# Attention of a decoder layer on one core: value products in pairs of groups, and an x load three groups later

## What is computed

```
x = layernorm(x + attention(x))          # 16 heads of 16, causal, w_qkv, w_proj
x = layernorm(x + slots(x, ctx_1024))    # 3 iterations of slot attention with a GRU cell
x = layernorm(x + experts(x))            # 16 experts of 64, the best 4 of them
```

```
qkv = x @ w_qkv + b_qkv                  # 16 heads, head dimension 16
att = einsum('bhqd,bhkd->bhqk', q, k) / 4, causal, softmax
y   = einsum('bhqk,bhkd->bhqd', att, v)
return y @ w_proj + b_proj
```

## Time and profile before

| | before |
|---|---|
| median of three runs | 658.3 us (658.2 to 659.8) |
| the profiled execution's own time | 656.96 us |
| its span (first to last instruction) | 655.2 us |
| TensorE busy | 616.9 us, 94% of the span |
| VectorE, ScalarE, GpSimd busy | 493.4, 327.1, 227.3 us |
| mean granted clock of TensorE | 0.993 of full speed |

### The profile page before, as it was taken

How to read it: one execution, slowest core, us unless ns; L and a number is a source line. 1 busy time by engine, 2 the same in 40 slices (tenths; PEclk the granted TensorE clock), 3 DMA queues, 4 the chain that set the end, 5 groups by cost and what they waited for, 6 DMA issues and landing times.

```text
span 655.2 us, 13948 instructions
## 1 busy us (share of the span) xinstructions
PE 616.9 (94%) x5048; PEld 561.9 (86%) x5064; DVE 493.4 (75%) x1039; ACT 327.1 (50%) x734; POOL 227.3 (35%) x274
## 2 busy tenths in 40 slices
PE   5889999999989899999999999999999997999996
PEld 5766787778768899999999999999988986999995
DVE  4755676666745888979888798897998988667663
ACT  5444645555664455664556645566466635131220
POOL 9502435233454431322323222232323114252542
PEclk9899999999999999999999999999999999899999
DMA  8645656457200400000000000000000000142250
GB/s 284 184 130 144 181 154 195 123 171 221 79 18 1 141 22 2 17 18 2 0 0 16 16 0 0 0 0 0 0 2 1 2 1 1 26 140 84 81 162 32
DMA packets 31374, 43.34 MB, mean 66 GB/s; under 512 B 3072, under 2 KB 18912, under 8 KB 31328
## 3 DMA queue, kind: packets, MB, share of 16 engines
q1 hardware_dynamic: 31328, 42.73, 21.5%
HBM read 29.39 MB, written 13.21 MB: 65 GB/s over the span
## 4 chain that ended last, share of the span: by engine, by line
PE 57%; DVE 15%; issue 13%; POOL 5%; DMA 4%; ACT 3%; SPq 2%; another core or an unknown queue 1%; DVEq 0%; POOLq 0%; ACTq 0%
PE bank L448 26%; PE bank L2163 11%; PE bank L1983 4%; POOL hid_hl L793 3%; PE bank L1883 2%; DMA k_rows<-k_hl 2%; PE bank L1841 2%; PE bank L1969 2%; PE bank L2000 1%; PE bank L456 1%; PE bank L1848 1%; PE bank L1864 1%; DMA k_op<-k_rows 1%; PE bank L1992 1%; DVE attn L1375 1%
## 5 line engine op out<-in xcount | busy, mean ns | idle before, releaser
L448 PE MATMUL bank<-slots_hl,whhT_hl 128*128 128x256 f32 x864 | 113.3, 284 | 0.0
L448 PEld LDWEIGHTS bank<-slots_hl,whhT_hl 128*128 128x128 f32 x864 | 105.7, 188 | 2.5 <-ACT gate_z L1096 1.0
L2163 PE MATMUL bank<-attn_hl,vg_hl 128*128 128x256 f32 x864 | 106.1, 281 | 0.2
L2163 PEld LDWEIGHTS bank<-attn_hl,vg_hl 128*128 128x128 f32 x864 | 101.2, 188 | 4.3 <-ACT attn_hl L807 3.9
L1285 DVE TENSOR_REDUCE neg_max<-bank 128x2 f32<-128x512 f32 (+1 forms) x96 | 65.5, 690 | 44.5 <-PE bank L1850 28.4
L862 ACT ACTIVATE pT<-bank 128x512 f32<-128x512 f32 x96 | 56.9, 598 | 47.2 <-PE bank L1864 31.6
L674 POOL TENSOR_SCALAR_AFFINE_SELECT pT<-pT 128x512 f32<-128x512 f32 x64 | 40.6, 638 | 107.3 <-ACT pT L862 107.2
L688 POOL TENSOR_TENSOR sq<-sq 128x256 f32<-128x256 f32 x24 | 18.1, 754 | 170.9 <-ACT sq L1081 130.4
L793 POOL TENSOR_TENSOR hid_hl<-hid,hid_hl 128x512 fp32r<-128x512 f32 x32 | 41.0, 1309 | 25.3 <-ACT hid_hl L807 25.2
L448 PE MATMUL bank<-values_hl,hid_hl 128*128 128x256 f32 x384 | 49.2, 286 | 0.3 <-DVE x L1559 0.3
L448 PE MATMUL bank<-x2T_hl,keys_hl 128*128 128x256 f32 x384 | 48.6, 284 | 0.0
(11 more groups left out here) (212 smaller groups left out, 1281.3 us busy)
## 6 DMA issues: line engine op xcount, KB each, us to landing
gate_rows<-gate_mem SPq DMA_DIRECT2D x48, 128.0 KB, 3.1
q_rows<-q_hl SPq DMA_DIRECT2D x21, 256.0 KB
k_rows<-k_hl SPq DMA_DIRECT2D x21, 256.0 KB
q_op<-q_rows SPq DMA_DIRECT2D x28, 192.0 KB, 3.2
k_op<-k_rows SPq DMA_DIRECT2D x14, 384.0 KB, 4.3
x_in<-in_x_dram SPq DMA_DIRECT2D x8, 256.0 KB, 6.6
c_in<-in_ctx_dram SPq DMA_DIRECT2D x8, 256.0 KB, 4.8
out_dram<-y_out SPq DMA_DIRECT2D x8, 256.0 KB, 2.8
```

The lines of the kernel that those rows point to most:

```text
L448: mm = pe.matmul(dst, left(a), right(b), start=first and n == 0, stop=last and n == 2, skip_group_check=True)
L2163: mm = pe.matmul(halves(b)[:, m, :], vg_hl[:, j, v_part, 3 * t + r, q:q + P], attn_hl[:, j, at_part, t, :], start=n == 2 and a + m + t == ...
```

## The change

On TensorE the value products of quads q and q + 1 (q even) are now both issued in third 1 of pass q + 2. Before, those of q came in third 2 of pass q + 1, and those of q + 1 in third 2 of pass q + 2. On SyncE the load of an even batch of x stands at place 3 of the period instead of place 0. On GpSimd the residual of an even batch stands at place 4 instead of place 3. Nothing else is changed, and the code's waits are the same.

```diff
@@ -559,7 +559,7 @@
                     write_q(period + 1, place // 2)
                 elif place in (1, 4) and 1 <= period + 1 < PAIRS:
                     write_k(period + 1, place // 4)
-                if place == 0 and 2 <= 2 * period < B:
+                if place == 3 and 2 <= 2 * period < B:
                     load_x(2 * period)
                 elif place == 5 and 2 <= 2 * period + 1 < B:
                     load_x(2 * period + 1)
@@ -737,7 +737,7 @@
                     text_lo(2 * (period + 2) + 1)
                 if 0 <= quad < QUADS:
                     causal(pT1[:, quad % 3, :, :], quad, 2)
-                if place == 3 and 0 <= 2 * period < B:
+                if place == 4 and 0 <= 2 * period < B:
                     residual(2 * period)
                 if place == 7 and 0 <= 2 * period + 1 < B:
                     residual(2 * period + 1)
@@ -2111,7 +2111,8 @@
                         natural(quad + LEAD, third)
                     if 0 <= quad < QUADS:
                         turned(quad, third)
-                    if third == 2 and 0 <= quad - 1 < QUADS:
+                    if third == 1 and quad % 2 == 0 and 0 <= quad - 2 < QUADS:
+                        heads(quad - 2)
                         heads(quad - 1)
                     for name, n in beside(quad, third):
                         work_beside(name, n)
```

## The result

The changed kernel took **665.7 us** (median of 4 runs, 663.4 to 667.4) beside 659.05 us for the kernel before on the same chip (658.2 to 660.8): ratio 1.0081, 95% interval 1.0043 to 1.0118. It is slower by 5.3 us (2.8 to 7.8) on the scale of the 658.3 us shown ahead. That scale puts after at 663.6 us, where 661.4 was predicted and the range went to 665.0: the sign is right, and the loss was put at 3.1 us, three fifths of its size. The profiled execution of after took 664.94 us (span 663.2), that of before 656.96 (655.2). These two are 8.0 us apart, more than the runs, because that of before is a short one.

What follows compares the result with a forecast made beforehand. TensorE, 94% busy, was taken as the bound, with the keys' way through DRAM and a GpSimd and VectorE chain. Terms summed to +3.1 us on the profiled 657.0, so 660.1, or 661.4 on the median's scale; range 655.7 to 665.0.

Steps and rivals of the forecast that it cites:

- A pair at 1.6 us: Value products on TensorE: a pair takes 1.6 us, saving 0.25 us; 16 pairs take 4.0 us off TensorE.
- Quad 8 at +0.1: Quads 4 to 8: residual ahead of x transposed loses the pairs' gain; quad 8 starts at +0.1 us (-0.5 to +0.4).
- Way of the keys to quads 12 and 20, taken at 0: k_op wait at quads 12 and 20: keys gain 1.1 to 1.9 us, lose 1.6 to the pair; taken as 0.
- the wait for k_op covers this: Odd quads between 8 and 12 and in 16 to 20: the k_op wait hides 0.5 to 1 us of ScalarE and VectorE pacing.
- Quad 12 to neg of quad 14, +2.5 us: GpSimd and VectorE chain: residual adds 1.4 us, the pair 1.1; TensorE's wait in quad 14 grows to about 4 us.
- From there to quad 16, -0.5 + 0.2: Quad 14 to 16: two pairs for four groups save 0.5 us; odd quads cost 0.2.
- Quads 16 to 24, 0 + 1.0: Way to quad 20 costs 0; to quad 24 the late load adds 1.0 us.
- which the longer wait at quad 24 covers: Quad 20: residual delays the deviation by 1.4 us and quad 22 by 1 to 2, hidden by quad 24's k_op wait.
- the load's term, +1.0: Late load_x traffic delays the keys for quad 24, lengthening the k_op wait there by 1.0 us (+0.3 to +1.9).
- The last quads, -0.2: Quads 24 to 32: pairs fill an exponential wait, residual and bare odd quads cost; -0.2 us (-1.5 to +1.0).
- Rival 1: Faster: TensorE sets the end, saved drains arrive and k_op waits vanish; 654.3 us, chance 0.18.
- Rival 3: Slower by more: x lands late behind write_q and GpSimd stands still in both periods; 664.5 us, chance 0.1.

Runs made afterwards that it cites:

- e5: Kernel before with value products in pairs behind the last scores of even quads, load_x and residual at their old places: 657.4 us, ratio 0.9953.
- e4: Changed kernel with the residual of even batches at place 6, behind the masking of quad 14, instead of place 4: 659.8 us, ratio 0.9986 to before.
- e1: Kernel before with only the value products in pairs in third 1, load_x and residual as before: 659.8 us, ratio 0.9992.
- e7: Changed kernel with load_x back at its old place 0, pairs and residual as in the change: 666.2 us, ratio 1.0088 to before.
- e2: Kernel before with only the residual of even batches moved from place 3 to place 4: 662.6 us, ratio 1.0020.
- e13: Kernel before with pairs behind the last scores and residual at place 6, load_x at its old place: 657.6 us, ratio 0.9951.
- e3: Kernel before with residual at place 4 and load_x at place 3, value products not paired: 664.6 us, ratio 1.0049.
- e10: Changed kernel with the pair behind the last scores in quads 4, 12, 20 and 28 only: 661.6 us, ratio 1.0017 to before.
- e12: Changed kernel with unread extra products on TensorE ahead of the neg transposes of quads 14 and 22: 669.4 us, ratio 1.0115 to before.
- e6: Kernel before with pairs behind the last scores, load_x at place 3 and residual at place 6: 657.6 us, ratio 0.9959.
- e8: Kernel before with load_x at place 3 and residual at place 6, value products not paired: 658.8 us, ratio 0.9969.

## Why the prediction was right in sign and short in size

The sum of its terms was +3.1 us; the ends of the stage lie 8.3 us apart in the two profiles (199.86 and 208.18). The runs are 5.3 us apart, so the terms below, read from one pair of executions, add up to more than the loss. Term by term, from the weight loads:

- **A pair at 1.6 us.** In after, from its first load to the next block's is 1.43 us, and entering takes 0.25: 1.68, so a pair saves 0.18 and not 0.25. By this the term was mis-sized by 1.1 us over 16 pairs. Entering varies with the block in front, from 0.13 to 0.35 us in before and in e5, so one price for all pairs is rough; at the pair of e5 (88.46) it is 0.14.
- **Quad 8 at +0.1.** This was right: 83.70 against 83.87. Quad 4's stretch loses 1.09 us, and e4, with residual away from it, only 0.12. Residual stands ahead of both low parts there, as argued; the second one ended at 74.15 and the projection started at 74.27, where 74.35 was forecast. Quad 4 had begun 1.1 us earlier, which pairs and start-up share.
- **Way of the keys to quads 12 and 20, taken at 0.** The landing became as short as forecast (6.95 us), but +0.52 and +0.55 us were lost. The step that failed is "the wait for k_op covers this" for the odd quads. In place of the k_op wait stand 1.08 us ahead of the first scores of quads 10 and 18, and 0.56 for y_nat in these quads. Both waits stand in e1 and e7 too, and there too no k_op wait is left at quads 12 and 20, with the load at its old place. So it isn't the load's leaving that removed the cover: TensorE itself comes later.
- **Quad 12 to neg of quad 14, +2.5 us.** This was right: 11.05 became 13.99, +2.94, by the chain described, with the wait at 4.26 against "about 4". The parts alone add up: +1.37 for residual (e2), where 1.4 was forecast, and +1.56 for the pair (e1), where 1.1 was.
- **From there to quad 16, -0.5 + 0.2.** This was wrong, and the largest miss: 10.61 became 12.25, +1.64 instead of -0.3. The prediction took every duration at full clock, though it forecast 4 us of an idle TensorE. At full clock the stretch takes 10.28 us (e5, e13), which is the forecast -0.3. With the clock at half level behind the wait, until 123.65, it took 1.97 us more; the projections alone took 2.21 instead of 1.22 us.
- **Quads 16 to 24, 0 + 1.0.** 20 to 24 lost 2.41 us, and not where forecast. There is no k_op wait at quad 24. Residual's delay of the deviation in quad 20, "which the longer wait at quad 24 covers", was covered by nothing: 1.30 us for k_op and 1.42 for y_nat in quad 22, then 3.41 us of half clock. e7, without the late load, lost as much (2.27), with one wait of 2.43 us for y_nat there. So the load's term, +1.0, stands for nothing that these runs show.
- **The last quads, -0.2.** The stretch took +0.30 in the table; that is within the bounds given.

Nearly all misses have one sign. The two covers that the prediction named were k_op waits, and TensorE's own new waits ahead of them left nothing to cover with. Rival 1 (drains arrive) failed for this change. The Trainium skill's rule (TensorEngine Tiling (Array Packing), Key Properties) that a change of tiling mode drains the engine agrees with the 0.20 us of idle behind every pair in after and in e5; e5, with half as many changes and nothing waiting behind the pair, is 3.1 us faster than before, some of it clock. Rival 3 (x late) is real in e3 and e10. In after the pair hid it at quad 12, and 0.39 us of it is left at quad 20.

The parts of this change are not additive: -0.5 us for the pairs and +1.3 for residual alone (each not to be told from nothing), +5.8 for the two together (e7). The long wait of quad 14 is not where they add to more than their sum: there they add up, and over 12 to 16 the two together (+4.81) are below the sum of e1 and e2 (+5.66), each of which has a half clock stretch of its own. In the table the excess stands in 4 to 8 (+1.12 against +0.36), in 20 to 24 (+2.27 against +0.51) and behind quad 24 (+0.31 against -0.60). How much of the loss is clock can be estimated from the runs: two half clock stretches more than in before, at 1.3 us each, are 2.6 us, about half of the 5.3. A second reckoning agrees with the price: among the 92 runs of before, a straight line through time and mean clock gives 1.4 us for 0.0026. The runs of before beside after have no clock on record, and why a stretch comes in one execution and not in the next stays open.

## What to carry to other kernels

When work is batched to save a fixed cost, place the batch behind everything in its step that others wait for; the same edit was worth -0.1% in the middle and -0.5% at the end. When a forecast gives a stall of over two microseconds on TensorE, price what follows it at half clock too; here a stretch of 3.41 us cost 1.3 us. And a wait that is counted as cover must be shown to be still there when the stall in front of it has made TensorE late.

## What the runs showed of the hardware that was not expected

- **The clock fell in or just behind waits of 2.2 to 4.3 us in a kernel in which TensorE is 93% busy.** Waits in quad 14 of 4.26 (after, e7) and 4.16 us (e3) came with 6.83 us at 1.2 GHz; 2.62, 2.71 and 2.87 us (e4, e2, e1) with 3.41 us, and so did 4.04 us (e10) and 4.26 us (e12). A wait of 2.23 us came with 3.41 us of it in e6 and none in e5; 2.25 us (e13), 2.17 us (e8, quad 22) and 1.33 us (before) came with none. So the same wait can cost differently from one execution to the next. The Trainium skill (TensorE: Matmul & The Clock Gate, Part 1: The HAM clock gate) says that the throttled state is the default and activity releases it. The traces agree: in after the clock fell at 116.82 with TensorE idle and was full again at 123.65, after 4.7 us of work.
- **Four residuals of 1.42 us on GpSimd, 5.7 us in all, cost 6.3 us** of the kernel's time (after against e4) where they stand in a chain that is already late, and 1.3 us or nothing (e2) where it is not.
